# Third attention: the output products of a group's second half are made in the next group, between its key rows and its weight-by-value products

## The reference, cut to what matters

```python
q = (query @ Wq).reshape(nb, q_len, H, D).transpose(0, 2, 1, 3)      # H = 32, D = 128
k = (key @ Wk).reshape(nb, q_len, KVH, D).transpose(0, 2, 1, 3)      # KVH = 8
v = (value @ Wv).reshape(nb, q_len, KVH, D).transpose(0, 2, 1, 3)
q = q * cos + _rotate_half(q) * sin
k = k * cos + _rotate_half(k) * sin
scores = jnp.einsum('bhqd,bhkd->bhqk', q, k) / jnp.sqrt(jnp.float32(D))
attn = jax.nn.softmax(jnp.where(mask == 0, -1000000000.0, scores), axis=-1)
x = jnp.einsum('bhqk,bhkd->bhqd', attn, v)
return x.transpose(0, 2, 1, 3).reshape(nb, q_len, H * D) @ Wo
```

## Time and profile before

| | us |
|---|---|
| median of 3 runs (lowest, highest) | 1994.57 (1985.47, 1994.76) |
| profiled execution, its own time | 1989.49 |
| its span, first to last instruction | 1988.2 |
| TensorE busy (share of the span) | 1691.7 (85%) |
| VectorE busy | 1120.8 (56%) |
| GpSimd busy | 684.2 (34%) |
| ScalarE busy | 507.9 (26%) |
| mean granted TensorE clock | 0.932 of full |

### The profile page before, as it was taken

The page is one execution under the profiler, slowest core; times in us unless marked ns, Lnnn a source line. Parts: engine busy times, 40 slices in busy tenths (PEclk is TensorE's granted clock), DMA queues, the critical chain, the costliest instruction groups (busy, mean ns, idle before and its releaser), DMA issues.

```text
span 1988.2 us, 19677 instructions
## 1 busy us (share of the span) xinstructions
PE 1691.7 (85%) x7898; PEld 1219.8 (61%) x7898; DVE 1120.8 (56%) x1550; ACT 507.9 (26%) x822; POOL 684.2 (34%) x452
## 2 busy tenths in 40 slices
PE   6761997999789959999999999997879667688998
PEld 2120665888548737777777776776554345546887
DVE  4999777223452445455554555555431288855666
ACT  3003001010421213232332332322121266542000
POOL 2665773121244303121331322211120266671221
PEclk9985998999889978899999999999889799988999
DMA  2000003100200021011010110101200311020000
GB/s 107 0 0 0 1 0 149 43 22 1 112 11 1 1 106 32 22 54 32 22 53 14 40 32 22 32 1 40 90 1 0 112 27 22 1 88 6 11 12 16
DMA packets 17579, 66.38 MB, mean 33 GB/s; under 512 B 1392, under 2 KB 9712, under 8 KB 13136
## 3 DMA queue, kind: packets, MB, share of 16 engines
q1 hardware_dynamic: 17488, 65.12, 9.4%
HBM read 58.82 MB, written 2.10 MB: 31 GB/s over the span
## 4 chain that ended last, share of the span: by engine, by line
PE 65%; DVE 20%; POOL 7%; ACT 3%; issue 2%; DMA 2%; SPq 0%; DVEq 0%; ACTq 0%; POOLq 0%
PE banks L269 38%; PE banks L263 21%; PE banks L364 3%; DVE arena L384 3%; POOL arena L1480 2%; DVE arena L1324 2%; POOL arena L1893 2%; DVE arena L233 1%; DVE arena L1783 1%; DVE arena L1790 1%; DVE arena L1782 1%; PE banks L1736 1%; DVE window L390 1%; ACT arena L1850 1%; POOL arena L1485 1%
## 5 line engine op out<-in xcount | busy, mean ns | idle before, releaser
L269 PE MATMUL banks<-grouped_split 128*128 128x512 f32 x1536 | 390.7, 408 | 11.7 <-DVE grouped_split L1352 8.4
L269 PEld LDWEIGHTS banks<-grouped_split 128*128 128x128 f32 x1536 | 291.7, 195 | 79.1 <-DVE grouped_split L1352 9.4
L1480 POOL TENSOR_TENSOR arena<-arena,grouped 128x512 f32<-128x512 f32 x80 | 105.0, 1316 | 403.4 <-ACT arena L1414 403.4
L263 PE MATMUL banks<-arena 128*128 128x64 f32 (+2 forms) x880 | 181.6, 427 | 46.8 <-DVE arena L384 27.4
L263 PEld LDWEIGHTS banks<-arena 128*128 128x128 f32 (+1 forms) x880 | 116.4, 188 | 122.2 <-issue 66.7
L269 PE MATMUL banks<-experts_split 128*128 128x512 f32 (+1 forms) x792 | 180.0, 389 | 1.9 <-DVE experts_split L578 1.9
L269 PEld LDWEIGHTS banks<-experts_split 128*128 128x128 f32 (+1 forms) x792 | 146.1, 185 | 35.1 <-DVE experts_split L575 2.1
L263 PE MATMUL banks<-dense 128*32 128x128 f32 (+6 forms) x970 | 133.9, 341 | 20.7 <-issue 9.4
L1320 DVE TENSOR_TENSOR arena<-banks,grouped 128x512 f32<-128x512 f32 x80 | 54.6, 683 | 170.2 <-ACT arena L1414 170.2
L364 PE MATMUL banks<-window_split 128*128 128x512 f32 x256 | 96.0, 499 | 45.6 <-DVE window_split L410 45.6
L263 PEld LDWEIGHTS banks<-dense 128*32 128x32 f32 (+3 forms) x970 | 91.2, 156 | 59.2 <-issue 37.9
(11 more groups left out here) (277 smaller groups left out, 3086.4 us busy)
## 6 DMA issues: line engine op xcount, KB each, us to landing
grouped<-in_attn SPq DMA_DIRECT2D x16, 1024.0 KB, 5.1
experts<-in_expert SPq DMA_DIRECT2D x8, 1024.0 KB, 4.8
dense<-in_w SPq DMA_DIRECT2D x2, 3584.0 KB, 13.1
linear<-in_ffn SPq DMA_DIRECT2D x1, 4096.0 KB, 15.7
grouped<-in_attn SPq DMA_DIRECT2D x8, 512.0 KB, 3.6
arena<-arena SPq DMA_DIRECT2D x16, 256.0 KB, 4.6
dense<-in_attn SPq DMA_DIRECT2D x1, 3072.0 KB, 12.4
arena<-in_x SPq DMA_DIRECT2D x1, 2048.0 KB, 7.6
```

The source lines that it names most:

```text
L263: return pe.matmul(dst, lhsT=lhsT, rhs=rhs, start=(k == 0), stop=(k == n - 1))
L269: s = pe.matmul(dst, lhsT=lhsT[i], rhs=rhs[j], start=(k == 0 and x == 0), stop=(k == n - 1 and x == 2))
L1480: g_.tensor_tensor(rot, rot, f(SIN + h * HALF, HALF), ALU.mult).then_inc(rot_sin.sem, 1)
```

## The change

The four output products of (g, 1) leave the end of group g and go into group g+1, behind its key rows (g+2, 0) and ahead of its weight-by-value products (g+1, 0). The last group's stay at the end. The split of the output weights (ScalarE's copy, VectorE's subtraction), which must not overwrite weights that these products still read, moves with them: from the start of a group to just ahead of `apply_high` and `apply_low` of its first half. The load of the next key and value weights waits for the value rows of the group before in place of its last output product.

```diff
@@ group_uses @@
         uses += [("q", g, q, 1) for q in range(QH2)] + [("v", g, h, 0) for h in range(2)]
-        uses += [("k", g + 1, 0, 0)] * nxt + [("a", g, 0, j) for j in range(4)]
+        uses += [("k", g + 1, 0, 0)] * nxt
+        uses += [("o", g - 1, t, 1) for t in range(4) if g] + [("a", g, 0, j) for j in range(4)]
         uses += [("q", g + 1, 0, 0)] * nxt + [("o", g, t, 0) for t in range(4)]
         uses += [("q", g + 1, 1, 0), ("q", g + 1, 2, 0)] * nxt + [("a", g, 1, j) for j in range(4)]
-        uses += [("q", g + 1, 3, 0), ("k", g + 1, 1, 0)] * nxt + [("o", g, t, 1) for t in range(4)]
-    return uses
+        uses += [("q", g + 1, 3, 0), ("k", g + 1, 1, 0)] * nxt
+    return uses + [("o", G2 - 1, t, 1) for t in range(4)]
@@ attn2, sync @@
-            sp.wait_ge(*use_mm(at_use["o", g - 1, 3, 1] + 1 if g else 6))
+            sp.wait_ge(*use_mm(at_use["v", g - 1, 1, 0] + 1 if g else 6))
@@ attn2, tensor @@
                 k_rows(g + 1, 0)
+            if g:
+                for t in range(4):
+                    output(g - 1, t, 1)
             apply(g, 0)
...
                 k_rows(g + 1, 1)
-            for t in range(4):
-                output(g, t, 1)
+        for t in range(4):
+            output(G2 - 1, t, 1)
@@ attn2, vector @@
-            v.wait_ge(*wo_hi(g + 1))
-            v.tensor_tensor(wos[1], f(STG_O, LQ), wos[0].bitcast(F32), ALU.subtract).then_inc(wo_lo.sem, 1)
             rotary(("q", g, 0, 1))
...
                 rotary(("k", g + 1, 0, 0))
+            if g:
+                for t in range(4):
+                    output_add(g - 1, t, 1)
+            v.wait_ge(*wo_hi(g + 1))
+            v.tensor_tensor(wos[1], f(STG_O, LQ), wos[0].bitcast(F32), ALU.subtract).then_inc(wo_lo.sem, 1)
             apply_low(g, 0)
@@ attn2, scalar @@
-            act.wait_ge(*o_in(16 * (g + 1)))
-            if g:
-                act.wait_ge(*use_mm(at_use["o", g - 1, 3, 1] + 1))
-            act.activation(wos[0], f(STG_O, LQ), ACT.Copy).then_inc(wo_hi.sem, 1)
             rotary(("q", g, 0, 1))
...
                 rotary(("k", g + 1, 0, 0))
+            act.wait_ge(*o_in(16 * (g + 1)))
+            if g:
+                act.wait_ge(*use_mm(at_use["o", g - 1, 3, 1] + 1))
+            act.activation(wos[0], f(STG_O, LQ), ACT.Copy).then_inc(wo_hi.sem, 1)
             apply_high(g, 0)
```

More of the change, by code:

```diff
@@ L1390, in vector @@
                 rotary(("k", g + 1, 1, 0))
-            for t in range(4):
-                output_add(g, t, 1)
+        for t in range(4):
+            output_add(G2 - 1, t, 1)
     def scalar(act):
```

## The result

The changed kernel took 2037.5 us (median of 4 runs, 2032.9 to 2040.3) against 1990.0 for the kernel before (4 runs, 1981.0 to 1994.8): a ratio of 1.0255, 95% interval 1.0227 to 1.0282. The quotient of the two medians by itself is 1.0239, inside that interval. The kernel is slower, by 50.7 us where the kernel before takes 1988. The forecast was 2037, in a range of 2006 to 2060. The profiled execution took 2040.3 us.

A forecast was written before the change was run, and what follows sets the result against it. The loop was taken to be bound by TensorE, so the change could move only its idle time and clock: 1989.5 + 19.6 (waits) + 28.2 (clock) = 2037 us, range 2006 to 2060.

The forecast's parts named there:

- The wait at the group's start: Groups 1 to 7: query rows wait uncovered for the key rows' rotary, 3.36 us each, +23.5 us.
- The wait inside the group: Groups 1 to 6: the 3.04 us bank wait goes, the split delays the first bank instead; -4.2 us in all.
- Group 0: No products to move, but the moved weight subtraction lands on the path of the first bank: +2.3 us.
- Group 7: The 2.61 us bank wait goes, the first output product then waits some 0.6 us: -2.0 us.
- Sum of the waits: Start, inside, group 0 and group 7 together: 23.5 - 4.2 + 2.3 - 2.0 = +19.6 us.
- The clock: TensorE falls to half clock behind both waits, two falls a group instead of one, 3.2 us each: +28.2 us.
- Waits without clock: Rival: the new waits come but bring the clock down no further; 2009 us, chance 0.12.
- The rival with the wait inside the group covered: First bank's low parts are made in time under the output products, no second new wait; 1989.5 us, chance 0.06.
- The rival of longer stretches: Each clock fall lasts as long as the one at 764; 2062 us or somewhat more, chance 0.03 beyond the band.

The follow-up runs named there:

- earlier rotary: Changed kernel with the wait ahead of a group's first query rows set on the last query rows' rotary, not the second half's key rows': 1991.2 us, 1.0010.
- control: Kernel before with only the wait ahead of a group's first query rows set on the last query rows' rotary: 1985.4 us, 0.9998.
- two filled kernels: 12 unused matmuls in each new wait of the changed kernel (1991.8 us), or in the kernel before's 3.04 us wait, groups 1 to 6 (1974.3 us).
- late split: Changed kernel with the split of the output weights behind the high and low parts of a group's first weight-by-value products: 2014.0 us, 1.0126.

## Why the prediction was right

*The wait at the group's start.* Forecast 3.36 us in seven groups, measured 3.40 in seven. The prediction named the rotary that the output products had covered; the earlier rotary takes it away, and the control shows that it was covered before. Right.

*The wait inside the group.* The 3.04 us went, and the split took its place, as forecast. The stretch from the first pair to the query rows was put at 5.35 us and measured 1145.58 - 1140.43 = 5.15, in place of 6.02: 6 x -0.87 = -5.2 us where -4.2 was forecast. Right, and ScalarE was more prompt than assumed (0.06 us behind the last output add, where the earlier trace rows have 0.34).

*Group 0.* From its first pair to the query rows 794.49 - 786.28 = 8.2 us passed, where in the kernel before it had been 798.34 - 793.49 = 4.9. That is +3.3 in place of the forecast +2.3, but 1.2 of it is not the moved L1381: the wait for the key rows' bank was 3.03 us in one trace and 1.86 in the other. Timelines of TensorE in group 0, the kernel before, the changed kernel, and the control (the kernel before with the earlier rotary):

```profile
796.49 1.13 PE L263 MATMUL banks<-grouped 64*128 64x256 f32 x8 [1.86 <-DVE arena L1320]
```

```profile
786.28 1.13 PE L263 MATMUL banks<-grouped 64*128 64x256 f32 x8
790.44 1.60 PE L263 MATMUL banks<-grouped 64*128 64x256 f32 x8 [3.03 <-DVE arena L1324]
794.49 1.62 PE L269 MATMUL banks<-grouped_split 128*128 128x512 f32 x3 [2.46 <-DVE grouped_split L1356]
```

```profile
789.90 1.13 PE L263 MATMUL banks<-grouped 64*128 64x256 f32 x8
794.06 1.14 PE L263 MATMUL banks<-grouped 64*128 64x256 f32 x8 [3.03 <-DVE arena L1320]
795.91 1.39 PE L269 MATMUL banks<-grouped_split 128*128 128x512 f32 x3 [0.71 <-DVE grouped_split L1352]
```

The control has the same order as the kernel before and a wait of 3.03 us; against its 795.91 - 789.90 = 6.0 us the change costs +2.2. The 1.86 came behind a stretch of 10.2 us at half clock at the group's start, which made TensorE late for the bank; in the changed kernel that stretch was 3.4 us. Right.

*Group 7.* The wait of 2.61 us went, and the 0.6 us that was to take its place did not come: -2.6 in place of -2.0. Its timeline in the changed kernel:

```profile
1399.92 2.08 PE L263 MATMUL banks<-grouped 64*128 64x256 f32 x16
1401.93 3.79 PE L263 MATMUL banks<-arena 128*128 128x64 f32 x32
1405.62 11.15 PE L269 MATMUL banks<-grouped_split 128*128 128x512 f32 x48
```

*Sum of the waits*: forecast +19.6 us; the parts measured add to 23.8 - 5.2 + 2.2 - 2.6 = +18.2, and the two filled kernels give +18.3 (uncertain by some 6). Both filled kernels have about 31 us at half clock left in the loop, so the difference is one of waits.

*The clock*: forecast +28.2, measured 44.9 - 12.5 = +32.4 (the filled kernels against theirs without fillers, uncertain by some 8), and 28.9 in the profiled executions. The sum was right, its parts less so. The falls were said to come in every group behind both waits and to cost 3.2 us each. In the changed kernel's trace five of seven start waits and five of six waits inside groups 1 to 6 had one, and they lasted from 3.4 to 17.0 us; the bound of 10.2 us for one was too low. Half the busy time of these stretches is 26.0 us at the starts, where 22.4 was forecast, and 24.9 inside the groups, which is 9.2 more than before, where 7.5 was. Against that stand -4.6 us in group 0, for which the sum had no term and whose two stretches happened to be short (3.4 and 10.2 us, where the kernel before had 10.2 twice). That the total came out near the choice was partly luck: the late split, with fewer waits, had seven longer stretches, and the same estimate missed it by 21 us.

*The rivals.* Waits without clock (2009) falls: with the waits kept and the idle time filled, 45 us went. What the changed kernel lost to its half clock in the loop, 119.6 / 2 = 60 us, is 2.9% of its span. The Trainium skill ("TensorE: Matmul & The Clock Gate", Part 1) says that for modelling the ramp to full clock is under 1% of a typical kernel's span and that a count of slow matmuls is not to be fitted. Read as the prediction read it, as a reason to leave the clock out, it would have missed by 28 us; the trace disagrees, with fourteen falls and those 60 us in one loop. The rival with the wait inside the group covered (1989.5) falls, since L1381 stood ahead of L1356 as the order said. The late split, which makes nearly that kernel, measured 2014 and not 1990: the rival left the clock behind the start waits at 3.2 us each, and it grew to 6.1, half of (699.75 - 614.36) / 7. The rival of longer stretches (2062 or more) did not come in the changed kernel as a whole, though five of its fourteen stretches lasted 13.6 or 17.0 us.

Not settled: what decides how long a stretch at half clock lasts. The wait at the start of group 0 is the same in nine of the ten kernels, 3.35 or 3.36 us with the same query rows and scores behind it, and the stretch at it lasted 3.4 us in four of them, 6.8 in one, 10.2 in one and 17.1 in three. The late split's seven all came at the same work and lasted 10.2 or 13.6 us; why two start waits of 3.40 us in the changed kernel had no fall was not tried.

## What to carry to other kernels

Work that is moved to cover one wait has been covering something where it stood: list the waits behind its old place, and what moves along with it, before asking what it hides at the new one. Read what each wait is for; here it asked for a result that only a later step reads, and with that put right and the dependent split moved behind the urgent one, the same move was worth 1.6% instead of costing 2.6%. In this loop a TensorE wait of some 3.4 us cost about twice its length where the clock fell behind it (2.45% for seven, 7 us each), so price a wait and its clock apart, with fillers if need be.

## What the runs showed of the hardware

Useless matmuls made a kernel faster. 156 of them in thirteen waits took 45 us off the changed kernel (1.0255 to 1.0029), 72 took 12.5 us off the kernel before, and 84 took 34 us off the late split.

The same wait is not always followed by the same time at half clock. In the profiled executions the seven start waits of 3.40 us brought 54.4 us at half clock with the other new wait in place and 88.4 us without it. By the times, the start waits cost 1.0255 - 1.0010 = 2.45% with the other in place and 1.0126 - 0.9838 = 2.88% without it, and the wait inside 1.29% beside the start waits and 1.72% alone. The difference of 0.43% points the same way, but is no larger than four intervals leave open (some 0.5%), so the times do not show it. Of these costs 1.2% (23.8 us) and some 0.7% (3.07 - 0.61 = 2.5 us in six groups) are the waits themselves; the rest is clock, but for 2.3 us in group 0.
